# An attention and mixture-of-experts layer on one core: two VectorE jobs moved to Pool, the turned maxima moved ahead of the projection unit

## The reference

```python
h = layernorm(x) * (1 + ca) + sa
x = x + ga * attention(h)        # 16 heads of 64
h = layernorm(x) * (1 + cb) + sb
x = x + gb * experts(h)          # 4 experts of 256, the best 2 of each token

def attention(X):
    Q, K, V = split(X @ W_qkv + b_qkv)
    P = softmax(Q K^T / 8)
    return (P V) @ W_fc + b_fc
```

## Time and profile before

| | us |
| --- | --- |
| median of 3 runs | 1880.54 |
| lowest, highest | 1879.64, 1888.0 |
| the profiled execution | 1879.13 |
| its span | 1877.4 |
| TensorE busy in it | 1631.7 |
| VectorE busy | 1255.0 |
| Pool busy | 1157.2 |
| ScalarE busy | 934.7 |
| mean granted TensorE clock | 0.96 |

### The profile page before, as it was taken

How to read it: one execution, slowest core, us unless ns; L and a number is a source line. 1 busy time by engine, 2 the same in 40 slices (tenths; PEclk the granted TensorE clock), 3 DMA queues, 4 the chain that set the end, 5 groups by cost and what they waited for, 6 DMA issues and landing times. The chain is left out here.

```text
span 1877.4 us, 29540 instructions
## 1 busy us (share of the span) xinstructions
PE 1631.7 (87%) x8907; PEld 856.8 (46%) x8907; DVE 1255.0 (67%) x2591; ACT 934.7 (50%) x1369; POOL 1157.2 (62%) x517
## 2 busy tenths in 40 slices
PE   3688999999999999999999999999999999946996
PEld 2344444444444444444444444444444444424886
DVE  5576666666666666666666666666666666468788
ACT  3354444455545454545555444444555545415874
POOL 3275667776666666767666676767776666711124
PEclk8699999999999999999999999999999999968999
DMA  2000000000000000000000000000000000020000
GB/s 86 17 22 28 24 29 28 28 13 27 28 28 28 28 28 23 28 28 28 28 28 28 28 28 25 26 28 28 28 12 28 28 28 25 15 78 23 30 34 28
DMA packets 60738, 54.40 MB, mean 29 GB/s; under 512 B 23678, under 2 KB 46747, under 8 KB 60699
## 3 DMA queue, kind: packets, MB, share of 16 engines
q1 hardware_dynamic: 60544, 53.90, 9.3%
q10 hardware_dynamic: 154, 0.03, 0.0%
HBM read 31.35 MB, written 2.36 MB: 18 GB/s over the span
## 5 line engine op out<-in xcount | busy, mean ns | idle before, releaser
L535 POOL TENSOR_TENSOR ACC<-ACC,PR 128x1024 f32<-128x1024 f32 x382 | 934.1, 2445 | 170.5 <-ACT PR L598 148.0
L642 DVE TENSOR_REDUCE NMH<-ps_mx 128x1 f32<-128x512 f32 x1024 | 658.5, 684 | 313.9 <-PE ps_mx L824 313.6
L598 ACT ACTIVATE PR<-ps_s 128x1024 f32<-128x1024 f32 x512 | 497.3, 1023 | 399.5 <-PE ps_s L848 396.2
L859 PE MATMUL ps_o<-PR,V 128*64 128x512 f32 x2048 | 517.0, 627 | 0.0
L824 PE MATMUL ps_mx<-KH,QH 64*128 64x512 f32 x1024 | 252.7, 488 | 133.0 <-DVE NMH L642 73.2
L535 POOL TENSOR_TENSOR ACC<-PR 128x1024 f32<-128x1024 f32 x64 | 151.6, 2369 | 342.3 <-ACT PR L598 342.3
L824 PEld LDWEIGHTS ps_mx<-KH,QH 64*128 64x128 f32 x1024 | 97.9, 185 | 380.1 <-issue 206.3
L859 PEld LDWEIGHTS ps_o<-PR,V 128*64 128x64 f32 x2048 | 127.6, 139 | 258.5 <-issue 195.2
L845 PE MATMUL ps_s<-QH,DL 64*128 64x512 f32 x1024 | 202.6, 389 | 0.0
L578 ACT ACTIVATE SUM<-ps_mx 128x512 f32<-128x512 f32 x64 | 38.2, 597 | 276.1 <-PE ps_mx L801 276.1
L842 PE MATMUL ps_s<-QH,DH 64*128 64x512 f32 x768 | 151.9, 392 | 0.0
(11 more groups left out here) (195 smaller groups left out, 1925.2 us busy)
## 6 DMA issues: line engine op xcount, KB each, us to landing
hcur<-hT SPq DMA_DIRECT2D x32, 512.0 KB, 3.3
SUM<-recip_rows SPq DMA_DIRECT2D x128, 128.0 KB, 2.8
Wraw<-in_L_attn_W_qkv SPq DMA_DIRECT2D x32, 192.0 KB, 2.9
x<-in_L_attn_X SPq DMA_DIRECT2D x4, 512.0 KB, 5.5
Wfc<-in_L_attn_W_fc SPq DMA_DIRECT2D x32, 64.0 KB, 1.8
R<-SUM SPq DMA_DIRECT2D x128, 2.0 KB, 1.7
hT<-in_L_attn_X SPq DMA_DIRECT2D x4, 512.0 KB, 6.4
out<-e_res SPq DMA_DIRECT2D x7, 256.0 KB, 2.3
```

The lines of the kernel that those rows point to most:

```text
L535: G.tensor_tensor(ACC[:, ch, :, :], a, PR[:, t, :, :], ALU.add).then_inc(added, 1)
L598: A.activation(PR[:, t, :, :], ps_s[:, t % 2, :, :], ACT.Exp, scale=SCALE).then_inc(exp_done, 1)
L642: D.tensor_reduce(NMH[:, ch, h, i, kc:kc + 1], ps_mx[:, h, :], AX, ALU.max, negate=True).then_inc(mx_red, 1)
L859: last = T.matmul(ps_o[half(h), :], V[:, u, t, half(h)], PR[:, t, h, :], start=(t == 0), stop=(t == 7))
```

## The change

`split_w` and `normalise` are removed from VectorE's steps and written for Pool: `normalise` for the previous pair behind the third add of each chunk, `split_w` behind the fifth add of the second chunk; at the stage's start Pool builds the first two low parts. VectorE keeps its `normalise` for the last pair. On TensorE, in steps 3 and 7, the turning moves from the end of the step to right behind the exact scores, ahead of the unit, and the second group of maxima moves from there to behind the unit, where it waits for the masked rows. On VectorE `mask_rows` moves to between the reductions of the first and the second group in steps 3 and 7, and `invert` from the head of steps 1 and 5 to the end of steps 0 and 4.

```diff
--- before.py
+++ after.py
@@ -394,8 +394,7 @@
 
         LATE = {0: ("k", 1, 0), 1: ("k", 1, 1), 2: ("q", 1, 0), 3: ("fc", -1, 0), 4: ("q", 1, 1), 5: ("v", 1, 0),
                 6: ("v", 1, 1), 7: ("fc", -1, 1)}
-        RECIP = {1: (-1, 0), 5: (-1, 1)}
-        NORM = {2: (-1, 0), 6: (-1, 1)}
+        RECIP = {0: 0, 4: 1}
         LAST_ON_POOL = 6
 
         def has(n):
@@ -513,7 +512,19 @@
         def _(pool):
             G = nc.gpsimd
 
+            def split_w(m, u):
+                pool.wait_ge(w_hi, m + 1)
+                for h in range(2):
+                    last = G.tensor_tensor(Wlo[:, :, h, :], Wraw[:, u, h, 0:2, :], Whi[:, :, h, :].bitcast(F32), ALU.subtract)
+                last.then_inc(w_lo, 1)
+
+            def normalise(m, ch):
+                pool.wait_ge(recip_in, 32 * (2 * m + ch + 1))
+                pool.wait_ge(o_copied, 2 * m + ch + 1)
+                G.tensor_tensor(O[:, ch, :], O[:, ch, :], SUM[:, ch, :], ALU.mult).then_inc(o_norm, 1)
+
             def first():
+                split_w(0, 0)
                 G.memset(one_r[:, :].bitcast(F32), 1.0).then_inc(s_init, 1)
                 G.memset(NM[:, :, :, :].bitcast(F32), 0.0).then_inc(s_init, 1)
                 G.memset(mask[:, :, :], 1.0).then_inc(s_mask, 1)
@@ -522,6 +533,8 @@
                 for h in range(2):
                     G.affine_select(out=mask[half(h), :, :], in_=mask[half(h), :, :], compare_op=ALU.is_equal, fill=0.0,
                                     base=0, pattern=[[-1, 4], [0, P]], channel_multiplier=1).then_inc(s_mask, 1)
+                pool.wait_ge(s_mask, 3)
+                split_w(1, 1)
 
             def pair(n, u):
                 for ch in range(2):
@@ -533,6 +546,10 @@
                         if t > 1:
                             pool.wait_ge(added, 7 * chunk + t - 1)
                         G.tensor_tensor(ACC[:, ch, :, :], a, PR[:, t, :, :], ALU.add).then_inc(added, 1)
+                        if t == 3 and has(n - 1):
+                            normalise(n - 1, ch)
+                        if t == 5 and ch == 1 and has(n + 2):
+                            split_w(n + 2, u)
 
             run(pool, pair, first)
 
@@ -627,12 +644,6 @@
         def _(dve):
             D = nc.vector
 
-            def split_w(m, u):
-                dve.wait_ge(w_hi, m + 1)
-                for h in range(2):
-                    last = D.tensor_tensor(Wlo[:, :, h, :], Wraw[:, u, h, 0:2, :], Whi[:, :, h, :].bitcast(F32), ALU.subtract)
-                last.then_inc(w_lo, 1)
-
             def reduce_max(m, u, ch, i, kc, count):
 
                 if i == 0 and kc == 0:
@@ -694,7 +705,6 @@
                 D.tensor_tensor(O[:, ch, :], O[:, ch, :], SUM[:, ch, :], ALU.mult).then_inc(o_norm, 1)
 
             def first():
-                split_w(0, 0)
                 dve.wait_ge(s_init, 2)
                 early_part("k", 0, 0, 0)
                 late_part("k", 0, 0, 0)
@@ -707,29 +717,24 @@
                         early_part("q", 0, 0, 1)
                 dve.wait_ge(s_mask, 3)
                 mask_rows(0, 0)
-                split_w(1, 1)
 
             def pair(n, u):
                 for d in range(8):
-                    if d % 4 == 0 and (d or has(n - 1)):
-                        mask_rows(n, d // 4)
-                    if d in RECIP and has(n + RECIP[d][0]):
-                        invert(n + RECIP[d][0], RECIP[d][1])
                     k = 2 * d + 9
                     if has(group(n, u, k)[0]):
                         reduce_max(*group(n, u, k), 16 * n + k)
                     x = late_at(n, u, d - 1)
                     if x:
                         late_part(*x)
+                    if d % 4 == 3 and has(group(n, u, k)[0]):
+                        mask_rows(group(n, u, k)[0], group(n, u, k)[2])
                     if has(group(n, u, k + 1)[0]):
                         reduce_max(*group(n, u, k + 1), 16 * n + k + 1)
                     x = late_at(n, u, d)
                     if x:
                         early_part(*x)
-                    if d in NORM and has(n + NORM[d][0]):
-                        normalise(n + NORM[d][0], NORM[d][1])
-                    if d == 6 and has(n + 2):
-                        split_w(n + 2, u)
+                    if d in RECIP and has(n - 1):
+                        invert(n - 1, RECIP[d])
                     if isinstance(n, int) and n == 1 and d < 6:
                         gate_rows(d)
 
@@ -902,12 +907,19 @@
                         maxima(*group(n, u, k), 16 * n + k)
                     scores(n, u, 2 * d)
                     scores(n, u, 2 * d + 1)
-                    if has(group(n, u, k + 1)[0]):
+                    turned = d % 4 == 3 and has(group(n, u, k)[0])
+                    if turned:
+                        wait(pe, mx_red, 2 * (16 * n + k + 1))
+                        rows(group(n, u, k)[0], group(n, u, k)[2])
+                    elif has(group(n, u, k + 1)[0]):
                         maxima(*group(n, u, k + 1), 16 * n + k + 1)
                     x = late_at(n, u, d)
                     if x:
                         freed(before(n, u, d))
                         unit(*x)
+                    if turned and has(group(n, u, k + 1)[0]):
+                        pe.wait_ge(neg_rows, 2 * n + (d + 1) // 4 + 1)
+                        maxima(*group(n, u, k + 1), 16 * n + k + 1)
                     if d:
                         times_v(n, u, 2 * d - 2)
                         times_v(n, u, 2 * d - 1)
@@ -916,10 +928,6 @@
                         times_v(n - 1, 1 - u, 15)
                     if sums_at(n, d):
                         sums(*sums_at(n, d), groups)
-                    if d % 4 == 3 and has(group(n, u, k)[0]):
-                        m, _, ch, _, _ = group(n, u, k)
-                        wait(pe, mx_red, 2 * groups)
-                        rows(m, ch)
 
             def last():
                 times_v(NP - 1, 1, 14)
```

## The result

| | before | with the change |
| --- | --- | --- |
| median, us | 1882.95 (4 runs) | 1806.93 (4 runs) |
| lowest to highest | 1879.64 to 1888.0 | 1802.01 to 1814.47 |
| ratio, 95% interval | | 0.9598, 0.9552 to 0.9643 |
| the profiled execution, its span | 1879.13, 1877.4 | 1810.36, 1808.6 |

The change makes the kernel 4.0% faster. The page of the changed kernel, against the earlier trace rows: TensorE does the same work in a shorter span, and VectorE's busy time has fallen by 146 us while Pool's has risen by only 71 us. The two read alike between set-up and router, so slices of 45 to 47 us don't show the short stretches at the low clock of the kernel before; narrow windows and the lengths of the pairs do.

A forecast was written before the change was run, and what follows sets the result against it. TensorE bounds the kernel, held up by VectorE in the attention stage. From 1879.1 us: 60 off for the pairs, 21 off for the low clock, 1 added for the stage's ends, giving 1799 us; range 1786 to 1828.

The forecast's parts named there:

- What bounds it: Attention stage: TensorE, busy 87% of the span, waits for VectorE's reduced maxima (2.0 us) and masked rows (0.8 to 1.1).
- the gap in step 7: TensorE idles 2.05 us between first and second maxima of step 7; the change removes it, gaining 2.00 us a pair.
- one delay of 4.4 us: VectorE before step 7's first maxima: normalising O (1.71 us) and W's low part (2.68) make their reduction late.
- The new order: TensorE, steps 3 and 7: masked-rows wait hidden behind the unit, some 0.7 us passing to ScalarE's copy; step 3 loses 0.06.
- The stretch from the first maxima to the next step: TensorE after the change: 7.26 us in step 3 (7.20 before), 7.55 in step 7 (9.55 before).
- The wait for ScalarE's copy: TensorE ahead of steps 0 and 4: the copy of the column sums takes over some 0.7 us of waiting.
- A net of 1.94 us a pair: Step 7 gains 2.00 us, step 3 loses 0.06; over 31 pairs 60 us.
- The low clock: TensorE at 1.2 GHz behind step 7's gap in 13 pairs, 1.6 us each; these 21 us go with the gap.
- a clock bound to step 7: Rival in the step 3 idle-task experiment: low clock periodic, tied to step 7 or nothing; none behind step 3, 1877 us; no chance given.
- the sign that I named: If right, no slice between the first and the last pair shows a granted clock below 9 tenths.
- the 1 us that I had put there: Last pair, Pool's adds on the path: two normalisations add about 1 us; +1 taken for both stage ends.
- The port shared by VectorE and Pool: Trainium skill's warning that moving work between the engines might not help; rival of no change, 1879 us, chance 0.02.

The follow-up runs named there:

- the two parts alone: Two kernels built on the changed one: both jobs on Pool with the order of before, 1798.8 us; the new order with both jobs on VectorE, 1893.7 us.
- early sums: The changed kernel with the column sums of steps 3 and 7 moved from behind the products with V to right behind the turning: 1766.57 us.
- the old order: The changed kernel with both jobs on Pool, but TensorE's and VectorE's order of turning, masked rows and second maxima as before: 1798.8 us.
- the fastest kernel: Changed kernel with second maxima ahead of the unit again, turning and column sums between the two blocks of products with V: 1747.82 us.

## Why the prediction was right

Forecast 1799 us, 1786 to 1828; measured 1806.93 at the median, 1810.36 in the profiled execution. Point by point:

- **What bounds it, and that the gap in step 7 goes: right.** Shown by the waits after, and by the two parts alone: without the jobs on Pool the gap stays.
- **Both jobs as one delay of 4.4 us: right as a sum, incomplete as a cause.** I did not say that either one could stay. The experiments show that, and why the sum (1.71 and 2.68) is so large: behind the normalisation W's low part sat out a whole add of Pool; without it, it takes 1.19.
- **The new order is worth nothing: right, with a small minus.** My sum has step 3 lose 0.06 us and takes step 7's gain from the jobs, with a new order that only swaps one wait for another. By the pairs with and without it the order costs 0.23 us, some 7 us in all.
- **The stretch from the first maxima to the next step:** 7.26 us forecast for step 3, 7.46 measured (610.96 to 618.42); 7.55 for step 7, 7.45 measured. The terms: turning starts after 2.17 us, not 2.08; turning takes 0.27 and 0.14, for my 0.20; unit 1.05 and maxima 0.43 as said; V 1.77; sums to next step 1.77 and 1.89, for 1.73 and 2.02. The wait for ScalarE's copy, forecast as some 0.7 us, is 0.74 to 0.87. The early sums show that it is that copy.
- **A net of 1.94 us a pair:** 1.8 measured, 5 us less over 31 pairs.
- **The low clock: right, on evidence that I had read in part wrongly.** 21 us forecast; 20 measured in the 28 pairs from pair 2 on. The gap as its cause is shown for the regular pairs by moving it to step 3 and by shortening it. But that the clock never falls elsewhere in a pair or behind step 3 is not true of the kernel before: in pair 1, step 3, TensorE waits 1.52 us, not at most 0.78, and the clock falls behind it:

```profile
143.66 0.50 PE L824 MATMUL ps_mx<-KH,QH 64*128 64x512 f32 x2 [1.52 <-DVE NMH L642]
...
146.00:148.00 2.00, 2.00 (x8) 0.53 (x6) 2.00 (x2) 0.00 (x0) 1.52 (x1) 0.50 0.00 0
```

That row already spoke against a clock bound to step 7. And the sign that I named, a slice below 9 tenths, could not have told right from wrong: no slice of the kernel before shows one between the first and the last pair either.

- **Pool: right.** Normalising 1.28 us (1.26), W's low part 0.45 each (0.43; a line through the two rows that I named, with 2.42 us for an add, gives 0.39, and 0.43 takes the 2.37 of the earlier trace rows). Nothing waits for O: no line of TensorE for o_norm. In the last pair Pool's chunks stand without a pause, and VectorE's adds of the last two blocks start at 1566.40, 17.4 us behind the first scores of the last chunk at 1548.99; before it was 16.4 (1640.81 and 1624.45). That is the 1 us that I had put there.
- **The port shared by VectorE and Pool.** The warning from the Trainium skill ("Perfetto Trace Analysis", Optimizing Scalar/DVE Operations), that moving work between the two might not help, is not borne out: VectorE's busy time fell by twice what Pool's rose, and Pool's 382 adds into ACC went from 934.1 us to 905.7, since nothing of VectorE's holds them up any more. With only the normalisation left on VectorE they take 931.2 us, with only W's low part 908.6: the two engines do hold each other up, and yet the move helped.
- **What is over:** 1810.4 less 1799 is 11 us; 5 are the pairs' length, 6 the stages behind the attention, which the change does not touch (315 to 329 us from pair 30 on, in eleven traces).

## What to carry to other kernels

An engine that feeds the bottleneck has a slack, and jobs put into it cost nothing until they exceed it together: measure the slack ahead of the deadline, and move one job before moving two. When a hand-written order is changed to cover one wait, look for the next release that the same instruction needs (here the copy of the sums behind the masked rows), and place both producers early enough; that was worth 51 us beside the old order and 59 beside the change's, and the reordering alone nothing. Two jobs that read two SBUF inputs are best kept out of each other's way on VectorE and Pool: here a short one that started during a long one ended only behind it. Keep products that run side by side on different parts of the array together.

## What was not expected of the hardware

- A lone product of 128x64 weights with 512 columns took 1.00 us, as long as each block of the two heads' products takes when it stands apart (0.96 and 1.01 in the fastest kernel's step 3).
- In the regular pairs the clock fell to 1.2 GHz behind gaps of 2.0 to 2.5 us, but only in about half of the cases (12, 16 and 17 of 27 pairs), and never behind one of 1.3 us or less. Outside them it also fell once behind 1.52 us, and once behind two waits of 1.17 and 0.78 us close together; it did not behind a gap of 1.60 us in pair 0 of the kernel before. The pairs with a fall are evenly spread: two or three pairs apart with the gap of 2.0 us, one or two apart with those of 2.3 and 2.4. Why one gap is followed by a fall and the next is not stays open.
- In the two places shown, a VectorE instruction with two inputs in SBUF that started during one of Pool's adds ended 0.15 us after that add: the same two subtractions took 2.68, 1.19 or, with no add running, 0.49 us.
